# Fused patch embedding, attention and experts: first transfers from two engines, bias and normalisation rows spread by TensorE, normalisation in two passes, weight splits reordered

## The reference, cut to what matters

```python
xp = input.reshape(B, C, H // P, P, W // P, P)                 # 8 images, 16x16 patches
x = einsum('bchpwq,dcpq->bhwd', xp, patch_w) + patch_b         # 512 tokens of 192
x = layernorm(x, ln_g, ln_b) + sinusoidal_pe                   # the stage that the change touches first
identity = x
x = gelu(x @ ff1_w + ff1_b) @ ff2_w + ff2_b                    # 192 -> 768 -> 192
x = windowed_attention(x, qkv_w, qkv_b, proj_w, proj_b) + identity
x = ff(x) + x
h = concatenate([x, txt])                                      # 96 tokens an image
h = h + selected_token_attention(layernorm(h))
h = h + sixteen_experts_and_a_shared_one(layernorm(h))         # top 4 of 16
```

## Time and profile before

| | us |
|---|---|
| median of 3 runs | 237.15 |
| lowest, highest | 237.05, 239.15 |
| profiled execution | 238.68 |
| its span, first to last instruction | 236.7 |
| busy in the span: PE, DVE, ACT, POOL | 222.0, 159.6, 110.9, 36.3 |

### The profile page before, as it was taken

The page is one execution under the profiler, slowest core; times in us unless marked ns, Lnnn a source line. Parts: engine busy times, 40 slices in busy tenths (PEclk is TensorE's granted clock), DMA queues, the critical chain, the costliest instruction groups (busy, mean ns, idle before and its releaser), DMA issues.

```text
span 236.7 us, 4330 instructions
## 1 busy us (share of the span) xinstructions
PE 222.0 (94%) x1470; PEld 192.9 (81%) x1470; DVE 159.6 (67%) x419; ACT 110.9 (47%) x220; POOL 36.3 (15%) x58
## 2 busy tenths in 40 slices
PE   7898988988999999999899999999999999999992
PEld 4677988865678988677587689899999999999991
DVE  0378996796731546454867679868787777878763
ACT  2057616165555355460203464546555565655542
POOL 6030059132501043303003000000000000000000
PEclk9999997999999999999999999999999999999998
DMA  6999000000000000003000000254544445454203
GB/s 188 338 407 257 16 1 3 0 3 1 0 0 3 0 0 3 0 1 91 0 3 0 0 0 20 82 191 138 178 128 131 144 152 152 153 155 133 85 0 100
DMA packets 10366, 19.27 MB, mean 81 GB/s; under 512 B 1456, under 2 KB 4800, under 8 KB 10352
## 3 DMA queue, kind: packets, MB, share of 16 engines
q1 hardware_dynamic: 10352, 19.09, 26.1%
HBM read 18.44 MB, written 0.64 MB: 81 GB/s over the span
## 4 chain that ended last, share of the span: by engine, by line
PE 69%; DVE 19%; ACT 4%; DMA 3%; issue 2%; POOL 1%; SPq 1%; DVEq 0%
PE bank L528 7%; PE bank L529 6%; PE bank L530 6%; PE bank L531 6%; PE bank L532 6%; PE bank L553 4%; DMA rows<-in_rows 3%; PE bank L671 2%; PE bank L988 2%; PE bank L994 2%; PE bank L998 2%; PE bank L989 2%; PE bank L990 2%; DVE act1s L1396 2%; PE bank L651 2%
## 5 line engine op out<-in xcount | busy, mean ns | idle before, releaser
L1291 ACT ACTIVATE hid_s<-hid 128x384 fp32r<-128x384 f32 x34 | 17.7, 524 | 24.2 <-DVE hid L1738 23.9
L553 PE MATMUL bank<-filler 128*128 128x512 bf16 x92 | 27.7, 400 | 1.3 <-POOL table L430 1.3
L1720 DVE SCALAR_TENSOR_TENSOR gated<-bank,expert_raw,silu 128x384 f32<-128x384 f32 x32 | 19.6, 615 | 7.7 <-PE bank L532 7.3
L1744 DVE TENSOR_TENSOR hid_s<-hid,hid_s 128x384 fp32r<-128x384 f32 x34 | 18.6, 553 | 9.1 <-ACT hid_s L1291 9.1
L1281 ACT ACTIVATE silu<-bank,expert_raw 128x384 f32<-128x384 f32 x34 | 19.6, 578 | 9.4 <-PE bank L532 9.3
L528 PE MATMUL bank<-tA,ug_w 128*128 128x384 f32 x68 | 23.2, 341 | 0.1
L531 PE MATMUL bank<-tB,ug_w 128*128 128x384 f32 x68 | 22.9, 337 | 0.0
L529 PE MATMUL bank<-tA,ug_w 128*128 128x384 f32 x68 | 22.9, 336 | 0.0
L530 PE MATMUL bank<-tA,ug_w 128*128 128x384 f32 x68 | 22.9, 336 | 0.0
L532 PE MATMUL bank<-tB,ug_w 128*128 128x384 f32 x68 | 22.9, 336 | 0.0
L1738 DVE TENSOR_TENSOR hid<-w_all,gated 128x384 f32<-128x384 f32 x30 | 16.6, 552 | 1.3 <-DMA w_all<-routing_weights 1.3
(11 more groups left out here) (303 smaller groups left out, 550.5 us busy)
## 6 DMA issues: line engine op xcount, KB each, us to landing
w_all<-routing_weights SPq DMA_DIRECT2D x15, 384.0 KB, 3.7
expert_raw<-in_experts SPq DMA_DIRECT2D x17, 256.0 KB, 3.7
expert_raw<-in_experts SPq DMA_DIRECT2D x17, 97.0 KB, 2.0
patches<-in_patches SPq DMA_DIRECT2D x3, 384.0 KB, 7.3
ff_raw<-in_ff SPq DMA_DIRECT2D x1, 768.0 KB, 7.4
kv_raw<-in_kv SPq DMA_DIRECT2D x1, 578.0 KB, 10.4
patch_w<-in_patch_w SPq DMA_DIRECT2D x2, 288.0 KB, 3.8
ff_raw<-in_ff SPq DMA_DIRECT2D x1, 576.0 KB, 7.5
```

Of the source, the lines that this page charges most:

```text
L553: mm(out[:, :], filler[:, 0:128], filler[:, :], start=True, stop=True)
L1291: a(hid_s[p][:, 0, H2N * hf:H2N * hf + H2N], hid[hf][:, :], ACT.Copy)\
L1720: v.scalar_tensor_tensor((hid if first else gated)[hf][:, :], bank[4 + 2 * hf][:, 0:H2N], expert_raw[:, p, BG:BG + 1], silu[hf][:, :], ALU ...
L1744: v.tensor_tensor(hid_s[p][:, 1, tok], hid[hf][:, :], f(hid_s[p][:, 0, tok]), ALU.subtract)\
```

## The change

- The first transfers are issued by two engines. SP issues the patches, then `cols`, the rest of `const`, `ff2`, `qkv` and on. ACT issues the patch weights, the first part of `const`, `rows` and `ff1`.
- `rows` is read as one line to partition 0 (the rest is set to zero by POOL). `top_row` is a 128x128 weight with ones in row 0 only (it borrows space in `kv_w`). A product with it adds `patch_b` to each tile's sum, and two products spread `ln_g` and `ln_b` to all partitions in banks 2 and 3; ACT copies `ln_g` out, and DVE adds `ln_b` from PSUM to the position.
- Moments are taken straight from PSUM. Normalisation is two passes: (x - mean) * `ln_g` (`token_centre`), and times the reciprocal root plus `bpe` (`token_scale`). Half of the `ff1` low part lies between the passes of half 0.
- `ff1`'s high part is made in two pieces. `patch(3)` moves behind `turn_x(0)`, and `turn_x(1)` ahead of the last product of `hidden1(0)`. Fillers: 7 to 6, 1 to 0, 9 to 3, 4 to 3.
- For half 1, three of the six copies in `split_hidden` move to ACT.
- DVE makes `bqm` early, and does the first two steps of `ff_out(0)` ahead of the `qkv` low part; the third step (`ff_out_low`) follows it.
- POOL starts `gate`, `bd` and `causal` only after `y_lo` 4, then `xpb`; the `kv` parts come after `x1b` of half 0.

```diff
 FILL = {
-    "patches": 7, "turn_x0": 1, "hidden0": 9, "turn_x1": 0, "hidden1": 4, "ff_out0": 0, "ff_out1": 0,
+    "patches": 6, "turn_x0": 0, "hidden0": 3, "turn_x1": 0, "hidden1": 3, "ff_out0": 0, "ff_out1": 0,
...
             for k, part in enumerate((slice(0, first), slice(first, PK))):
-                sp.dma_start(patch_w[:, part, :], d["patch_w"][:, part, :]).then_inc(d_pw[k], 16)
                 sp.dma_start(patches[:, 0, part], d["patches"][0][:, part]).then_inc(d_patch0[k], 16)
-            sp.dma_start(patches[:, 1], d["patches"][1]).then_inc(d_patch[1], 16)
-            sp.dma_start(rows[:, 0:ROWS_FIRST], d["rows"][:, 0:ROWS_FIRST].to_broadcast([128, ROWS_FIRST]))\
-                .then_inc(d_rows, 16)
-            sp.dma_start(patches[:, 2], d["patches"][2]).then_inc(d_patch[2], 16)
-            sp.dma_start(const[:, 0:CONST_FIRST], d["const"][:, 0:CONST_FIRST]).then_inc(d_const, 16)
-            sp.dma_start(patches[:, 3], d["patches"][3]).then_inc(d_patch[3], 16)
-            sp.dma_start(ff1_raw[:, :], d["ff1"]).then_inc(d_ff1, 16)
+            for t in range(1, 4):
+                sp.dma_start(patches[:, t], d["patches"][t]).then_inc(d_patch[t], 16)
...
             step, after = chain(gp, "gp_step")
+            top_row = f(kv_w[:, 0, 0:128])
...
             g.memset(ones[:, :], 1.0).then_inc(s["filler_done"], 1)
+            k = step(g.memset(top_row, 0.0))
             step(g.memset(minus_half[:, :], -0.5))
+            after(k)
+            g.memset(top_row[0:1, :], 1.0).then_inc(s["filler_done"], 1)
+            g.memset(rows[:, 0:ROWS_FIRST], 0.0).then_inc(s["filler_done"], 1)
...
                 rsqrt(ve1, mv1, rs1, 2 * hf, 2 * hf + 2, 128, "rs_done")
-            gp.wait_ge(d_rows2, 16)
-            gp.wait_ge(s["act1_lo"], 2 * FK)
-            for hf in range(2):
-                gp.wait_ge(s["x_done"], hf + 1)
-                t = slice(2 * hf, 2 * hf + 2)
-                g.tensor_tensor(xpb[:, t, :], x[:, t, :],
-                                row("proj_b", 0, 128).unsqueeze(1).to_broadcast([128, 2, DIM]), ALU.add)\
-                    .then_inc(s["xpb_done"], 1)
...
+            gp.wait_ge(s["y_lo"], 4)
             gp.wait_ge(d_kv, 48)
-            k = step(g.tensor_scalar(kv_w[:, 0, :], kv_raw[:, :], 1.0, 1.0, ALU.mult, ALU.mult))
-            after(k)
-            g.tensor_tensor(kv_w[:, 1, :], kv_raw[:, :], f(kv_w[:, 0, :]), ALU.subtract)\
-                .then_inc(s["small_split"], 1)
...
+            gp.wait_ge(d_rows2, 16)
+            for hf in range(2):
+                gp.wait_ge(s["x_done"], hf + 1)
+                t = slice(2 * hf, 2 * hf + 2)
+                g.tensor_tensor(xpb[:, t, :], x[:, t, :],
+                                row("proj_b", 0, 128).unsqueeze(1).to_broadcast([128, 2, DIM]), ALU.add)\
+                    .then_inc(s["xpb_done"], 1)
...
                     .then_inc(s["x1b_done"], 1)
+                if hf == 0:
+                    k = step(g.tensor_scalar(kv_w[:, 0, :], kv_raw[:, :], 1.0, 1.0, ALU.mult, ALU.mult))
+                    after(k)
+                    g.tensor_tensor(kv_w[:, 1, :], kv_raw[:, :], f(kv_w[:, 0, :]), ALU.subtract)\
+                        .then_inc(s["small_split"], 1)
...
             mm, tr = nc.tensor.matmul, nc.tensor.transpose
+            top_row = f(kv_w[:, 0, 0:128])
...
                         pe.wait_ge(d_patch0[k // (PK // 2)], 16)
-                    last = mm(bank[4 * (t // 2) + t % 2][:, 0:DIM], patches[:, t, k, :], patch_w[:, k, :],
-                              start=(k == 0), stop=(k == PK - 1))
-                last.then_inc(s["patch_ps"], 1)
+                    mm(bank[4 * (t // 2) + t % 2][:, 0:DIM], patches[:, t, k, :], patch_w[:, k, :],
+                       start=(k == 0), stop=False)
+                pe.wait_ge(d_rows, 16)
+                mm(bank[4 * (t // 2) + t % 2][:, 0:DIM], top_row, row("patch_b", 0, 128), start=False,
+                   stop=True).then_inc(s["patch_ps"], 1)
...
-            def hidden1(hf):
-                hidden(hf, hf + 1, (1, 2, 3), "gelu_done", "hid1_ps")
+            def hidden1(hf, products=range(FK)):
+                hidden(hf, hf + 1, (1, 2, 3), "gelu_done", "hid1_ps", products)
...
             keep_busy("patches", bank[7])
+            pe.wait_ge(s["filler_done"], 5)
             patch(0)
+            for k, name in enumerate(("ln_g", "ln_b")):
+                mm(bank[2 + k][:, 0:DIM], top_row, row(name, 0, 128), start=True, stop=True)\
+                    .then_inc(s["spread_ps"], 1)
...
             patch(2)
-            patch(3)
...
             turn_x(x, 0, "x_done", bank[2], bank[3])
+            patch(3)
...
             pe.wait_ge(s["ff1_lo"], 1)
-            hidden1(0)
+            hidden1(0, range(0, 5))
...
             turn_x(x, 1, "x_done", bank[6], bank[7])
+            hidden1(0, range(5, FK))
...
             keep_busy("turn_h0", bank[0])
-            pe.wait_ge(s["small_split"], 1)
+            pe.wait_ge(s["small_split"], 3)
...
-            pe.wait_ge(s["small_split"], 2)
+            pe.wait_ge(s["small_split"], 3)
...
-            def gelu(hf, banks, ready, done):
-                for m in range(FK):
+            def gelu(hf, banks, ready, done, products=range(FK)):
+                for m in products:
...
                       bias=col("ff1_b", 128, m)).then_inc(s[done], 1)
+                    if done == "gelu_done" and hf == 1 and m % 2:
+                        act.wait_ge(s["gelu_done"], FK + m + 1)
+                        a(act1s[:, 1, 0, m, :], act1[:, 1, m, :], ACT.Copy).then_inc(s["act1_hi"], 1)
...
+            first = PK // 2
+            for k, part in enumerate((slice(0, first), slice(first, PK))):
+                act.dma_start(patch_w[:, part, :], d["patch_w"][:, part, :]).then_inc(d_pw[k], 16)
+            act.dma_start(const[:, 0:CONST_FIRST], d["const"][:, 0:CONST_FIRST]).then_inc(d_const, 16)
+            act.wait_ge(s["filler_done"], 5)
+            act.dma_start(rows[0:1, 0:ROWS_FIRST], d["rows"][:, 0:ROWS_FIRST]).then_inc(d_rows, 16)
+            act.dma_start(ff1_raw[:, :], d["ff1"]).then_inc(d_ff1, 16)
             load_table(ACT.Gelu_apprx_tanh, 0)
+            act.wait_ge(s["spread_ps"], 1)
+            a(row("ln_g", 0, 128), bank[2][:, 0:DIM], ACT.Copy).then_inc(s["gain_done"], 1)
             act.wait_ge(d_ff1, 16)
-            a(ff1_w[:, 0, :], ff1_raw[:, :], ACT.Copy).then_inc(s["ff1_hi"], 1)
+            for columns in (slice(0, FF // 2), slice(FF // 2, FF)):
+                a(v3(ff1_w[:, 0, :], FF)[:, :, columns], v3(ff1_raw[:, :], FF)[:, :, columns], ACT.Copy)\
+                    .then_inc(s["ff1_hi"], 1)
...
             act.wait_ge(d_cols, 32)
-            gelu(0, (1, 2, 3), "hid1_ps", "gelu_done")
+            gelu(0, (1, 2, 3), "hid1_ps", "gelu_done", range(0, 5))
             turned_hi(1, 2, bank[6], bank[7])
+            gelu(0, (1, 2, 3), "hid1_ps", "gelu_done", range(5, FK))
...
                 dve.wait_ge(s["patch_ps"], t + 1)
-                k = step(v.tensor_tensor(x0[:, t, :], bank[4 * (t // 2) + t % 2][:, 0:DIM],
-                                         row("patch_b", 0, 128), ALU.add))
-                after(k)
-                k = step(v.bn_stats(st1[:, t, :], x0[:, t, :]))
+                k = step(v.bn_stats(st1[:, t, :], bank[4 * (t // 2) + t % 2][:, 0:DIM]))
...
-            def token_norm(hf, kb):
-                ts = slice(2 * hf, 2 * hf + 2)
+            def token_centre(hf):
                 dve.wait_ge(s["mv1_done"], 2 * hf + 2)
+                for t in (2 * hf, 2 * hf + 1):
+                    k = step(v.scalar_tensor_tensor(x0[:, t, :], bank[4 * (t // 2) + t % 2][:, 0:DIM],
+                                                    mv1[:, t, 0:1], row("ln_g", 0, 128), ALU.subtract, ALU.mult))
+                return k
...
+            def token_scale(hf, k):
...
+                after(k)
...
                 for t in (2 * hf, 2 * hf + 1):
-                    k = step(v.tensor_scalar(x0[:, t, :], x0[:, t, :], mv1[:, t, 0:1], rs1[:, t:t + 1],
-                                             ALU.subtract, ALU.mult))
-                after(k)
-                k = step(v.tensor_tensor(x0[:, ts, :], x0[:, ts, :],
-                                         row("ln_g", 0, 128).unsqueeze(1).to_broadcast([128, 2, DIM]), ALU.mult))
-                after(max(k, kb))
-                v.tensor_tensor(x[:, ts, :], x0[:, ts, :], bpe[:, :].unsqueeze(1).to_broadcast([128, 2, DIM]),
-                                ALU.add).then_inc(s["x_done"], 1)
+                    last = v.scalar_tensor_tensor(x[:, t, :], x0[:, t, :], rs1[:, t:t + 1], bpe[:, :],
+                                                  ALU.mult, ALU.add)
+                last.then_inc(s["x_done"], 1)
...
                     dve.wait_ge(s["gelu_done"], i + 1)
-                    k = step(v.tensor_copy(act1s[:, hf, 0, m, :], act1[:, hf, m, :]))
-                    after(k)
+                    if hf == 1 and m % 2:
```

(41 more changed lines are left out.)

## The result

| us | before | after |
|---|---|---|
| median (each of 5 runs) | 237.15 | 235.04 |
| lowest, highest | 237.0, 239.15 | 233.17, 235.4 |
| ratio, 95% interval | | 0.987 (0.983 to 0.991) |
| a second time, on another chip: median | 237.62 | 233.77 |
| ratio there | | 0.987 (0.984 to 0.990) |

The kernel is faster by 1.3%, about 3.1 us; 233.7 was forecast, with 231.9 to 235.7 as the range. Ratios leave out executions more than 1.5% above the fastest of their kernel, among them one of 748.58 us of the kernel before and one of 363.76 of `before_pool_late`. The profiled one belongs to the lower group, and the profiled one of before held a stretch at 1.2 GHz, so for a comparison like for like before was traced again.

What follows compares the result with a forecast made beforehand. Bound by the `rows` broadcast and transfer order up to 24 us, then PE's wait for DVE before the queries; gains 0.3 (head) + 1.6 (stage end) + 1.5 (clock) = 3.4 off 237.15 gave 233.7, range 231.9 to 235.7.

Steps and rivals of the forecast that it cites:

- What bounds the kernel: Up to 42 us: the `rows` broadcast landing at 9.85, and about 2.0 us of idle PE before the queries.
- Time of `x_done(0)`: Head, normalisation of half 0: moments end at 12.4, `x_done` at 14.9 against 14.74 before, no gain.
- if SP's side moves as much meanwhile: First transfers: with equal sharing, 1472 KB landed at about 8.8, less the dropped broadcast's part; `rows` taken at 8.3.
- `ff1` in time: Head: `ff1` lands at 12.6, DVE can go on at 13.35, agreeing with `x_done` at 14.9 within 0.1.
- rival (b): Head: `ff1` lands no earlier than before, at 14.2, making `x_done` 1.8 late; time 235.5, chance 0.13.
- rival (c): Head: `ff2` and `qkv` pass `ff1`, landing about 17.4; `x_done` 5.0 late, time 238.7, chance 0.04.
- `x_done` to P: PE from half 0 normalised to half 1's first product: first product of half 0 at 18.6, half 1 at 23.7, gain 0.3.
- End of the stage: PE's wait before the queries falls from 2.0 to 0.3 us, gain 1.6.
- The clock: After the shorter idle before the queries, no fall to half speed between 36.7 and 40.2; worth 1.5 us.
- The `kv` parts, `bqm`, POOL's own work at P + 13: Moved `kv` parts cost nothing, `bqm` 0.1 to 0.2; POOL's work from 13 us after half 1's first product precedes `prob` scaling.
- Rival (d): `rows` land by 8.0, `x_done` by 13.8, and the wait before the queries vanishes: 1.1 + 0.3 more, 232.3; chance 0.14.

Runs made afterwards that it cites:

- `before_pool_late`: Kernel before with one edit: POOL's `xpb` and all after it wait for `y_lo` 4 instead of the split of the hidden layer; 236.51 us, ratio 0.994.
- `before_rep`: Kernel before, nothing altered, run again for a second trace; median 238.07 us, ratio 1.002, traced execution 237.41.
- `before_fill`: Kernel before with eight filler products put into TensorE's wait before the queries; 237.6 us, ratio 1.000.

## Why the prediction came out right, and which steps failed

- *What bounds the kernel.* Right in both places: the chain entered by `rows`, and the stage ended on DVE held up by POOL.
- *Time of `x_done(0)`.* Wrong: 14.9 forecast, 13.56 measured (13.65 to 14.06 in four other traces). The failed step is "if SP's side moves as much meanwhile", priced at before's rate: rows at 8.3, tile 0 at 8.0. Both were in by 7.11 (`rows` by 7.55 in the latest trace), because the transfers without a broadcast, on two queues, moved 411 and not 285 GB/s. For tile 0 it was the second queue: with one queue and no broadcast its second half still came at 6.97. That error is 12.4 - 11.18 = 1.2 at the moments, and the DVE chain behind them took 2.38 for the 2.5 forecast.
- *`ff1` in time.* Right that it does not hold DVE; by the same error the landing was 10.26, not 12.6. With it rival (b) and rival (c) fell by far.
- *`x_done` to P.* 8.8 forecast (3.7 to H, then 5.1), measured 8.57 (3.35 and 5.22). Right.
- *End of the stage.* Right in size: P + 11.05 and a gain of 1.6 forecast, P + 11.08 and 1.63 measured. The reason was half right: the earlier copies and the order of DVE were counted, and the runs show that POOL's later start does all of it by itself.
- *The clock.* Wrong: 1.5 was taken from one execution that had the fall, as its consequence of the idle. `before_rep` had the idle without the fall, and `before_fill` a fall elsewhere without the idle. It was also taken off the wrong number: the execution with the fall took 238.68, and the median of 237.15 from which the 1.5 was subtracted is about what `before_rep` took without one (237.41).
- *The `kv` parts, `bqm`, POOL's own work at P + 13.* Right (POOL starts at 35.50 or P + 13.4 and ends `xpb` at 40.47, before its first scaling at 43.17); the gain at 42 us is all there at 84 (3.7 and 3.7).

Like for like the terms were 2.07 + 1.63 + 0 where 0.3 + 1.6 + 1.5 stood: 3.7 for 3.4, or, with the head's 1.6 by the means of all traces, 3.2. A head mis-sized by 1.3 to 1.8 too little and a clock by 1.5 too much nearly cancel. The sum was good because of two errors of opposite sign, not because each step was: that was luck. The median of 235.04 lies 1.3 above the forecast since four of those five executions fell in the upper group, most likely the later rise of the clock, which could not be read from one trace. Rival (d) was the one that named the mechanism (rows in time, `x_done` 13.8); it had the head, and it too kept the 1.5.

## What to carry to other kernels

When a change shortens or removes a transfer and spreads the first ones over two queues, forecast landings with the rate as a free term with two ends, not with the rate of before; a broadcast of a short line to 128 partitions deserves its own price. Before reordering an engine that looks late, see whether its small instructions end when another engine's long one does: here one wait on POOL gave what the edits of DVE and ACT were counted for. A clock fall in one trace is a term of the sum only if a second trace of the same kernel has it too.

## What was not expected of the hardware

- With the same first transfers to move, one queue gave 325 GB/s (one trace) and two gave 411 (408 to 411 in five traces) in the same six microseconds, at a DMA share near 1 in both; later one queue reached 429 to 434. The share of busy time of the DMA engines does not show how fast they are.
- The broadcast of 2.25 KB to 128 partitions pulled the rate down to 214 GB/s while it lasted.
- A DVE instruction of 0.35 to 0.42 us took up to 2.71 beside a long POOL one with both operands in SBUF, and ended 0.28 after it both times. A step of DVE that reads PSUM (0.48, L1404) was not slowed beside the same POOL instruction, and a 128x1152 one that had begun before POOL's was not either (1.35): there POOL waited.
- With the same code, TensorE reached 2.4 GHz at about 5.7 us in one execution and after 9 in others, and the clock column did not show it; the spacing of equal instructions did (0.16 and 0.32). It moved the end of the first moments by 1.9 and 2.4 us.
